# Decoder layer on one core: the down product of the seventh expert cut in two around the first gates of the eighth, and the last biases placed between the halves of the last down product

## The chip, the core and the metric

The kernel runs on one NeuronCore of a Trainium2 chip. The core has a matrix engine (TensorE, PE in the profile; its weight loads are listed as PEld), a vector engine (VectorE, DVE), a scalar engine (ScalarE, ACT), a general engine (GpSimd, POOL) and a queue that issues the DMAs (SyncE, SP). The metric is the time of one execution on the device in microseconds, as the median of repeated runs.

## What is computed

A decoder layer over 4 sequences of 256 tokens with 256 features: a state-space mixer, a small gate from a context, and then a feed-forward layer with experts. Only the last part matters here. For the layer-normed tokens `xt` (1024 of them) it is

```python
u = jnp.einsum('nh,ehi->eni', xt, Wup) + bup[:, None, :]
g = jax.nn.silu(jnp.einsum('eni,eij->enj', u, Wgate) + bgate[:, None, :]) * u
eo = jnp.einsum('enj,ejh->enh', g, Wdown) + bdown[:, None, :]
out = jnp.einsum('ne,enh->nh', probs, eo)
su = xt @ Wsu + bsu
sg = jax.nn.silu(su @ Wsg + bsg) * su
out = out + sg @ Wsd + bsd
```

There are 7 routed experts, of which each token weighs two with `probs`, and one shared expert that all tokens use. The kernel treats the shared one as an eighth (`NE` is 8, numbers 0 to 7), and runs every expert on every token.

## The kernel before

**Three products for an expert.** Up, gate and down are each a 256 by 256 product on 1024 tokens. Every 32-bit operand is split in a rounded high part and the rest of it (`uh` and `ul`, `eh` and `el`, `ewh` and `ewl` for weights), and a product is the sum of three passes: high by high, and the two mixed ones. Up and gate work on four blocks `v`, two halves of the tokens (512 each) by two halves of the features. A block is 6 matmuls of 512 columns into bank `v` (L1241 for the four with the high part of the moving side, L1244 for the two with the rest). Block 0 and block 1 belong to the first 512 tokens. Both need `uh` and `ul` of blocks 0 and 1 of the up product, because the gate sums over all features. Down works on eight tiles `t` of 128 tokens, 6 matmuls of 256 columns each (L1251), two tiles to a bank, banks 4 to 7.

**What the other engines do for one expert.** ACT adds the bias to the up result (`u32`, L909). DVE rounds it (`uh`, L1208), POOL subtracts (`ul`, L647). After the gate, ACT applies silu (`e32`, L930), DVE multiplies by `u32` (L1220), ACT rounds (`eh`, L925, in `round_e`), and POOL subtracts (`el`, L652). In the last expert DVE makes two of the four `el` blocks, 1 and 3 (L1225), to spare POOL, and POOL 0 and 2. DVE adds each down tile, weighed by `prob`, to the residual `xres` (`accumulate`, L1199), and the last expert's with L1191. In the profile `e32` and `u32` have the name `conv`, and `eh` the name `parts`, after the memory they lie in.

**The order of the work.** Each engine has its program in an order written out by hand, and waits on counting semaphores. The matrix engine's expert `e` is: up of `e`, down of `e - 1`, gate of `e`. Down of the last expert follows alone, and opens its banks with the weighed biases of all experts (8 matmuls, L1599), for which `acc_done` must show that the bank's tiles of the expert ahead have been added. `eh` has one buffer: `round_e` waits until the whole down product of the expert ahead has been read (`down_done` at `4 * e`). The down product of the last expert waits, at its tile 0 and its tile 4, for the two `el` blocks of that half (`el_done` from POOL, `el_last` from DVE). The output leaves in four DMAs, each after two tiles of L1191.

Of the kernel before, what the change touches and what calls it, by code (L numbers as in the profile page):

```python
# [56 lines left out]
def decoder_layer(nc, x, ctx_in, W_in, conv_w, conv_b, D, z_bias, W_out, xw, xb, Wr, br, gate_bias,  # L57
# [9 lines left out]
    with ExitStack() as stack:  # L67
# [597 lines left out]
        def _(act):  # L665
# [226 lines left out]
            def expert(e, k, q):  # L892
                first = isinstance(e, int) and e == 0
                if isinstance(e, int) and e == NE - 2:
                    for i in range(2):
                        act.wait_ge(prob_turned, i + 1)
                        act.copy(biasT[i], bank[4 + i][0:BIAS_ROWS, :]).then_inc(prob_read, 1)  # L897
                act.wait_ge(eb_done, e + 1)
                for v in range(4):
                    if first and v == 1:  # L900
                        root(slice(T + 4, 2 * T), 5)
                    if first and v == 2:
                        copy_logits(0)
                        split_turned(6, 6)
                        split_turned(7, 7)
                        act.preload_act_table(ACT.Silu)
                    act.wait_ge(up_done, 4 * e + v + 1)
                    at_least(act, e_done, 4 * (e - 1) + v + 1)
                    act.activation(u32[:, v, :], up_bank(e, v)[:], ACT.Identity,  # L909
                                   bias=eb[q][:, 0, v % 2:v % 2 + 1]).then_inc(up_read, 1)  # L910
                    if first:
                        act.wait_ge(up_read, v + 1)
                        act.copy(uh[:, v, :], u32[:, v, :]).then_inc(uh_done, 1)  # L913
                if first:
                    copy_logits(1)
                elif not (isinstance(e, int) and e == NE - 1):
                    at_least(act, down_done, 4 * e)
                    act.wait_ge(ew_in[1 - q], 48 * (k + q + 1))
                    for j in range(3):
                        split_weights(e + 1, 1 - q, j)  # L920

                def round_e(v):
                    act.wait_ge(e_done, 4 * e + v + 1)
                    at_least(act, down_done, 4 * e)
                    act.copy(eh[:, v, :], e32[:, v, :]).then_inc(eh_done, 1)  # L925

                for v in range(4):
                    act.wait_ge(gate2_done, 4 * e + v + 1)
                    at_least(act, el_done, 4 * (e - 1) + v + 1)
                    act.activation(e32[:, v, :], up_bank(e, v)[:], ACT.Silu,  # L930
                                   bias=eb[q][:, 1, v % 2:v % 2 + 1]).then_inc(silu2_done, 1)
                    if v:
                        round_e(v - 1)
                round_e(3)
                if first:

                    act.wait_ge(pexp_in, 1)
                    act.activation(lg[:], lg[:], ACT.Tanh).then_inc(pexp_done, 1)
# [5 lines left out]
        def _(dve):  # L944
# [247 lines left out]
                                             scalar=shift[:, t:t + 1], in1=xres[:, t, :],  # L1192
                                             op0=ALU.add, op1=ALU.add).then_inc(acc_done, 1)

            def accumulate(e):

                for t in range(T):
                    dve.wait_ge(down_done, 4 * e + t // 2 + 1)
                    dve.scalar_tensor_tensor(out=xres[:, t, :], in0=bank[4 + t // 2][:, DM * (t % 2):DM * (t % 2 + 1)],  # L1199
                                             scalar=prob[:, t, bass.ds(e, 1)], in1=xres[:, t, :],  # L1200
                                             op0=ALU.mult, op1=ALU.add).then_inc(acc_done, 1)

            def expert(e, k, q):
                first, second, final = (isinstance(e, int) and e == i for i in (0, 1, NE - 1))
                for v in range(4 * (not first)):
                    dve.wait_ge(up_read, 4 * e + v + 1)
                    at_least(dve, gate2_done, 4 * e)
                    dve.tensor_copy(uh[:, v, :], u32[:, v, :]).then_inc(uh_done, 1)  # L1208
                if not first:
                    accumulate(e - 1)  # L1210
                if not (first or final):
                    if second:
                        dve.wait_ge(ewl_done, 6)
                    for j in range(3):
                        rest_weights(e + 1, 1 - q, j)
                for v in range(4):
                    if first and v == 2:
                        compare()
                    dve.wait_ge(silu2_done, 4 * e + v + 1)
                    dve.tensor_tensor(e32[:, v, :], e32[:, v, :], u32[:, v, :], ALU.mult).then_inc(e_done, 1)  # L1220
                    if final and v >= 2:

                        w = 2 * v - 3
                        dve.wait_ge(eh_done, 4 * e + w + 1)
                        dve.tensor_tensor(el[:, w, :], e32[:, w, :], f32(eh[:, w, :]), ALU.subtract).then_inc(el_last, 1)  # L1225
                if first:
                    choose()
                    weigh_experts()
# [7 lines left out]
        def _(pe):  # L1236
# [353 lines left out]
                    high_first(up_bank(e, v)[:], [(w[q][:, 1, k, c], uh[:, 2 * n + k, :]) for k in range(KD) for w in (ewh, ewl)],  # L1590
                               [(ewh[q][:, 1, k, c], ul[:, 2 * n + k, :]) for k in range(KD)], before).then_inc(gate2_done, 1)

            def down(e, q):
                pe.wait_ge(ewl_done, 3 * e + 3)
                end = isinstance(e, int) and e == NE - 1
                for t in range(T * end):
                    if t % 2 == 0:
                        pe.wait_ge(acc_done, T * (e - 1) + t + 2)
                    pe.matmul(bank[4 + t // 2][:, DM * (t % 2):DM * (t % 2 + 1)], biasT[t // 4][:, t % 4 * P:(t % 4 + 1) * P], bd3[:],  # L1599
                              start=(t % 2 == 0), stop=False)  # L1600
                for t in range(T):
                    n = t // 4
                    if t % 4 == 0 and isinstance(e, int) and e == NE - 1:
                        pe.wait_ge(el_done, 4 * e + n + 1)
# [37 lines left out]
            def expert(e, k, q):  # L1642
                if isinstance(e, int) and e == 0:
                    up(0, 0, range(2))
                    logits(0)
                    turn_tokens(6, 6)
                    turn_tokens(7, 7)
                    gate(0, 0, range(2))
                    pe.wait_ge(lgT_read, 1)
                    up(0, 0, range(2, 4))  # L1650
                    logits(1)
                    turn_logits()
                    gate(0, 0, range(2, 4))
                else:
                    if isinstance(e, int) and e == NE - 2:
                        pe.wait_ge(acc_done, T * (NE - 3))
                        turn_prob()
                    up(e, q)
                    if isinstance(e, int) and e == NE - 2:
                        pe.wait_ge(prob_read, 2)  # L1660
                        pe.wait_ge(bd_done, 1)
                    down(e - 1, 1 - q)
                    gate(e, q)

            over_experts(pe, expert)
            down(NE - 1, 1)


# [27 lines left out]
```

## Time and profile before

| | us |
|---|---|
| median of 3 runs | 415.57 |
| lowest and highest | 415.22, 416.32 |
| profiled execution, its time | 417.49 |
| profiled execution, its span | 415.8 |

| engine | busy us | share of the span |
|---|---|---|
| PE | 392.3 | 94% |
| DVE | 333.7 | 80% |
| ACT | 227.4 | 55% |
| POOL | 176.8 | 43% |

The rows of the trace are times in us from the start of the span. The profiled execution took 1.69 us more than its span, for what lies around it, and was 1.92 us slower than the median of the unprofiled runs, so a change is reckoned as a difference in the span and laid on either time. The whole change lies in the last 22 us, from 393.7.

### The profile page before, as it was taken

The page shows a single profiled execution, that of the slowest core. Times are in us where ns is not written, and L with a number is a line of the kernel's source. Part 1 is how long each engine was busy: PE and PEld are TensorE (multiplying, and loading weights), DVE is VectorE, ACT ScalarE, POOL GpSimd, SP SyncE. Part 2 cuts the span into 40 slices and gives each one's busy share as a digit, 9 for nine tenths or more (in the row PEclk, how much of TensorE's full clock was granted, in tenths as well). Part 3 has the DMA queues.
Part 4 walks back from the last instruction along what each step waited for, and adds up shares of the span by engine and source line. Part 5 has one row for each costly group of instructions (what it writes and reads, how often), then busy time and mean ns, then how long its engine had stood idle before and what let it go on. Part 6 is the DMA issues. An engine that isn't in the chain of part 4 may idle for free.

```text
span 415.8 us, 8825 instructions
## 1 busy us (share of the span) xinstructions
PE 392.3 (94%) x2989; PEld 289.5 (70%) x2989; DVE 333.7 (80%) x565; ACT 227.4 (55%) x421; POOL 176.8 (43%) x208
## 2 busy tenths in 40 slices
PE   2899999999999999998999999599999999999996
PEld 1677666666667666664666667368897888978886
DVE  3687998999899998998988939819959678596685
ACT  5657455555555555558876631354555545555451
POOL 3699411011110111105546740226575865768561
PEclk9999999999999999999999999889999999999999
DMA  6402211322101221014231150000022020200002
GB/s 185 105 2 56 64 58 10 107 61 61 47 20 55 60 61 57 18 51 135 60 87 44 47 154 9 2 0 2 1 77 56 23 76 0 76 0 2 0 1 102
DMA packets 35932, 21.13 MB, mean 51 GB/s; under 512 B 17048, under 2 KB 33760, under 8 KB 35904
## 3 DMA queue, kind: packets, MB, share of 16 engines
q1 hardware_dynamic: 35904, 20.78, 17.7%
q8 instruction: 15, 0.25, 0.3%
q14 instruction: 13, 0.11, 0.1%
HBM read 18.13 MB, written 1.31 MB: 47 GB/s over the span
## 4 chain that ended last, share of the span: by engine, by line
PE 60%; DVE 18%; ACT 7%; issue 6%; POOL 5%; DMA 1%; DVEq 1%; ACTq 0%; SPq 0%; POOLq 0%
PE bank L1275 21%; PE bank L1468 7%; PE bank L1251 6%; POOL el L652 5%; PE bank L1388 4%; DVE conv L1012 4%; PE bank L1241 4%; DVE xres L1199 4%; PE bank L1456 3%; DVE conv L1220 2%; DVE ewl L1080 2%; PE bank L1261 2%; PE bank L1476 2%; PE bank L1415 2%; PE bank L1244 2%
## 5 line engine op out<-in xcount | busy, mean ns | idle before, releaser
L1012 DVE SCALAR_TENSOR_TENSOR conv<-bank,taps,conv 128x510 f32<-128x510 f32 (+2 forms) x204 | 150.8, 745 | 22.4 <-ACT conv L691 17.5
L1275 PE MATMUL bank<-uth,parts 128*128 128x512 f32 x272 | 96.7, 411 | 2.1 <-DVE utl L995 1.4
L691 ACT ACTIVATE conv<-bank,tap_b,taps 128x512 f32<-128x512 f32 x68 | 52.9, 778 | 57.3 <-PE bank L1275 57.2
L565 POOL TENSOR_TENSOR ce<-conv,ecx 128x512 f32<-128x512 f32 x15 | 19.4, 1295 | 123.1 <-DVE conv L1012 122.7
L1275 PEld LDWEIGHTS bank<-uth,parts 128*128 128x128 f32 x272 | 51.1, 188 | 16.3 <-DVE conv L1012 4.4
L647 POOL TENSOR_TENSOR ul<-conv,uh 128x512 fp32r<-128x512 f32 x32 | 42.9, 1358 | 42.3 <-ACT uh L913 29.3
L652 POOL TENSOR_TENSOR el<-conv,parts 128x512 fp32r<-128x512 f32 x30 | 44.3, 1504 | 30.3 <-ACT parts L925 30.3
L1275 PE MATMUL bank<-utl,parts 128*128 128x512 f32 x136 | 56.4, 415 | 0.0
L1208 DVE CAST uh<-conv 128x512 fp32r<-128x512 f32 x28 | 26.0, 967 | 22.5 <-ACT conv L909 22.3
L1095 DVE SCALAR_TENSOR_TENSOR g<-dec,bank 128x512 f32<-128x512 f32 x64 | 40.9, 679 | 1.7 <-PE bank L1388 1.7
L1220 DVE TENSOR_TENSOR conv<-conv 128x512 f32<-128x512 f32 x32 | 31.4, 1014 | 13.0 <-ACT conv L930 13.0
L1468 PEld LDWEIGHTS bank<-conv 64*128 64x128 f32 x512 | 31.1, 187 | 13.5 <-issue 11.1
L1468 PE MATMUL bank<-conv 64*128 64x128 f32 x512 | 37.2, 285 | 0.2
L1251 PE MATMUL bank<-ewh,parts 128*128 128x256 f32 x128 | 36.1, 282 | 0.7 <-ACT wzl L897 0.5
L1251 PE MATMUL bank<-ewl,parts 128*128 128x256 f32 x128 | 36.1, 282 | 0.0
L1251 PE MATMUL bank<-ewh,el 128*128 128x256 f32 x128 | 36.1, 282 | 0.0
L799 ACT ACTIVATE dec<-bank 128x512 f32<-128x512 f32 x64 | 34.5, 592 | 0.6 <-DVE g L1095 0.6
L925 ACT CAST parts<-conv 128x512 fp32r<-128x512 f32 x32 | 19.8, 618 | 27.6 <-DVE conv L1220 27.6
L1275 PEld LDWEIGHTS bank<-utl,parts 128*128 128x128 f32 x136 | 25.6, 189 | 8.6 <-issue 6.3
L909 ACT ACTIVATE conv<-bank,eb 128x512 f32<-128x512 f32 x32 | 19.7, 689 | 16.8 <-POOL eb L644 11.9
L930 ACT ACTIVATE conv<-bank,eb 128x512 f32<-128x512 f32 x32 | 21.9, 687 | 9.9 <-PE bank L1244 9.9
L1388 PE MATMUL bank<-g,xp 128*16 128x128 f32 x512 | 26.6, 278 | 0.0
(206 smaller groups left out, 732.1 us busy)
## 6 DMA issues: line engine op xcount, KB each, us to landing
w_raw<-in_L_attn_W_in_dram SPq DMA_DIRECT2D x17, 256.0 KB, 3.2
ecx<-ecum_dram SPq DMA_DIRECT2D x32, 128.0 KB, 2.9
ew_raw<-in_L_ffn_Wup_dram SPq DMA_DIRECT2D x7, 256.0 KB, 3.3
ew_raw<-in_L_ffn_Wgate_dram SPq DMA_DIRECT2D x7, 256.0 KB, 3.3
ew_raw<-in_L_ffn_Wdown_dram SPq DMA_DIRECT2D x7, 256.0 KB, 3.6
xres<-in_x_dram SPq DMA_DIRECT2D x2, 512.0 KB, 4.1
out_dram<-xres SPq DMA_DIRECT2D x4, 256.0 KB, 2.2
yi<-yev SPq DMA_DIRECT2D x56, 16.0 KB, 1.8
```

Source lines behind the costliest of these rows:

```text
L647: pool.tensor_tensor(ul[:, v, :], u32[:, v, :], f32(uh[:, v, :]), ALU.subtract).then_inc(ul_done, 1)
L652: pool.tensor_tensor(el[:, v, :], e32[:, v, :], f32(eh[:, v, :]), ALU.subtract).then_inc(el_done, 1)
L691: act.activation(conv[q][:, j, HALF * h:HALF * (h + 1)], bank[u % 2][:], ACT.Identity, bias=tap_b[q][:, j:j + 1], scale=taps[q][:, j, TAPS ...
L799: act.activation(dec[b][:], bank[4 + b][:], ACT.Exp).then_inc(exp_done, 1)
L1012: dve.scalar_tensor_tensor(out=dst[:, :, d:SEQ], in0=src[:, :, 0:SEQ - d], scalar=taps[q][:, j, TAPS - 1 - d:TAPS - d], in1=dst[:, :, d:SE ...
L1095: dve.scalar_tensor_tensor(out=g[b][:], in0=dec[b][:], scalar=1.0, in1=cb_bank(n, u // 2, b)[:], op0=ALU.min, op1=ALU.mult).then_inc(g_don ...
L1208: dve.tensor_copy(uh[:, v, :], u32[:, v, :]).then_inc(uh_done, 1)
L1220: dve.tensor_tensor(e32[:, v, :], e32[:, v, :], u32[:, v, :], ALU.mult).then_inc(e_done, 1)
L1251: ins = pe.matmul(dst, left, right, start=(k == 0 and i == 0 and not begun), stop=(ends and k == n - 1 and i == 2))
L1275: ins = pe.matmul(bank[u % 2][:], w, x_t, start=(i == 0), stop=(i == 3 * KD - 1))
L1388: ins = pe.matmul(y_bank(n, h)[32 * i:32 * i + 2 * HD, P * h:P * (h + 1)], xp[q][:, 4 * h + i, j, :], g[j][:, i * P:(i + 1) * P], start=fi ...
L1468: ins = pe.matmul(cb_bank(n, h, j)[:, i * P:(i + 1) * P], conv[q][r, 0, s], conv[q][r, 1, s], start=True, stop=True)
```

## The change

In the last expert (7), the down product of expert 6 is cut in two. The matrix engine now runs tiles 0 to 3 of it, the gate blocks 0 and 1 of expert 7, tiles 4 to 7, the biases of tiles 0 to 3, and then the gate blocks 2 and 3. The biases of tiles 4 to 7 move behind the first half of the last down product. The other engines follow. DVE adds the tiles 0 to 3 of expert 6 ahead of its products for the gate and the tiles 4 to 7 behind its first `el` block. It makes that block (1) ahead of the second half's products, where it stood behind the product of block 2. ACT rounds blocks 0 and 1 in a row and then 2 and 3 in a row, each pair behind the second silu of its half. No instruction is added or dropped.

```diff
@@ scalar engine, expert @@
+                    final = isinstance(e, int) and e == NE - 1
-                    if v:
+                    if v and not (final and v == 2):
                         round_e(v - 1)
+                    if final and v == 1:
+                        round_e(1)
                 round_e(3)
@@ vector engine @@
-            def accumulate(e):
-                for t in range(T):
+            def accumulate(e, tiles=range(T)):
+                for t in tiles:
                     dve.wait_ge(down_done, 4 * e + t // 2 + 1)
...
-                if not first:
+                if final:
+                    accumulate(e - 1, range(4))
+                elif not first:
                     accumulate(e - 1)
...
-                    if final and v >= 2:
-                        w = 2 * v - 3
+                    if final and v % 2:
+                        w = v
                         dve.wait_ge(eh_done, 4 * e + w + 1)
                         dve.tensor_tensor(el[:, w, :], e32[:, w, :], f32(eh[:, w, :]), ALU.subtract).then_inc(el_last, 1)
+                        if w == 1:
+                            accumulate(e - 1, range(4, T))
@@ matrix engine @@
+            def down_biases(tiles):
+                for t in tiles:
+                    if t % 2 == 0:
+                        pe.wait_ge(acc_done, T * (NE - 2) + t + 2)
+                    pe.matmul(bank[4 + t // 2][:, DM * (t % 2):DM * (t % 2 + 1)], biasT[t // 4][:, t % 4 * P:(t % 4 + 1) * P], bd3[:],
+                              start=(t % 2 == 0), stop=False)
...
-            def down(e, q):
+            def down(e, q, tiles=range(T)):
...
-                    down(e - 1, 1 - q)
-                    gate(e, q)
+                    if isinstance(e, int) and e == NE - 1:
+                        down(e - 1, 1 - q, range(4))
+                        gate(e, q, range(2))
+                        down(e - 1, 1 - q, range(4, T))
+                        down_biases(range(4))
+                        gate(e, q, range(2, 4))
+                    else:
+                        down(e - 1, 1 - q)
+                        gate(e, q)
...
-            down(NE - 1, 1)
+            down(NE - 1, 1, range(4))
+            down_biases(range(4, T))
+            down(NE - 1, 1, range(4, T))
```

The matrix engine in the last expert, before, from the last matmul of the seventh expert's down product. Bank 7 holds its tiles 6 and 7, banks 0 and 1 the gate blocks 0 and 1:

```order
L1251 MATMUL bank7<-ewh0,el 128x256
L1241 MATMUL bank0<-uh,ewh1 128x512 [waits uh_done,up_read,ewl_done]
L1241 MATMUL bank0<-uh,ewl1 128x512
L1241 MATMUL bank0<-uh,ewh1 128x512 [waits uh_done]
L1241 MATMUL bank0<-uh,ewl1 128x512
L1244 MATMUL bank0<-ul,ewh1 128x512 [waits ul_done] x2
L1241 MATMUL bank1<-uh,ewh1 128x512 [waits up_read]
```

The same gate in the changed kernel, with what stands ahead of it and behind it:

```order
L1258 MATMUL bank5<-ewh0,el 128x256
L1248 MATMUL bank0<-uh,ewh1 128x512 [waits uh_done,up_read,ewl_done]
L1248 MATMUL bank0<-uh,ewl1 128x512
L1248 MATMUL bank0<-uh,ewh1 128x512 [waits uh_done]
L1248 MATMUL bank0<-uh,ewl1 128x512
L1251 MATMUL bank0<-ul,ewh1 128x512 [waits ul_done] x2
L1248 MATMUL bank1<-uh,ewh1 128x512 [waits up_read]
L1248 MATMUL bank1<-uh,ewl1 128x512
L1248 MATMUL bank1<-uh,ewh1 128x512
L1248 MATMUL bank1<-uh,ewl1 128x512
L1251 MATMUL bank1<-ul,ewh1 128x512 x2
L1258 MATMUL bank6<-ewh0,parts 128x256 [waits acc_done,el_done,ewl_done]
```

The gate blocks 0 and 1 now stand behind bank 5, the first half of the down product, and banks 6 and 7 behind them.

The vector engine in the last expert, before. Banks 4 to 7 at L1199 are the tiles of expert 6, `conv1` is `e32`:

```order
L1199 SCALAR_TENSOR_TENSOR xres<-bank6,prob,xres 128x256 [waits down_done] x2
L1199 SCALAR_TENSOR_TENSOR xres<-bank7,prob,xres 128x256 [waits down_done] x2
L1220 TENSOR_TENSOR conv1<-conv1,conv0 128x512 [waits silu2_done] x3
L1225 TENSOR_TENSOR el<-conv1,parts 128x512 [waits eh_done]
L1220 TENSOR_TENSOR conv1<-conv1,conv0 128x512 [waits silu2_done]
L1225 TENSOR_TENSOR el<-conv1,parts 128x512 [waits eh_done]
```

And in the changed kernel (L1202 is the weighed addition, L1225 now the product, L1230 the subtraction for `el`):

```order
L1225 TENSOR_TENSOR conv1<-conv1,conv0 128x512 [waits silu2_done] x2
L1230 TENSOR_TENSOR el<-conv1,parts 128x512 [waits eh_done]
L1202 SCALAR_TENSOR_TENSOR xres<-bank6,prob,xres 128x256 [waits down_done] x2
L1202 SCALAR_TENSOR_TENSOR xres<-bank7,prob,xres 128x256 [waits down_done] x2
L1225 TENSOR_TENSOR conv1<-conv1,conv0 128x512 [waits silu2_done] x2
L1230 TENSOR_TENSOR el<-conv1,parts 128x512 [waits eh_done]
```

The last four weighed additions moved from ahead of all four products to between the second and the third, behind the first `el`.

## Rows read from the trace of the kernel before

**Rows 1.** The page: its span, and the engines on the chain that ended last.

```profile
span 415.8 us, 8825 instructions
...
PE 60%; DVE 18%; ACT 7%; issue 6%; POOL 5%; DMA 1%; DVEq 1%; ACTq 0%; SPq 0%; POOLq 0%
```

**Rows 2.** The chain that ended last, in order of time: start, us, what.

```profile
403.87 0.70 ACT conv L930
...
405.60 0.62 DVE el L1225
...
406.35 5.96 PE bank L1251 x48
...
412.33 0.48 DVE xres L1191
```

**Rows 3.** Timeline of PE, at 269 and from 393 on: start, us, operation, count, [idle].

```profile
269.55 1.97 PE L1291 MATMUL bank<-ident,xn 128*128 128x128 f32 x8 [4.67 <-DVE xn L988]
...
393.75 0.28 PE L1251 MATMUL bank<-ewh,parts 128*128 128x256 f32 x1
...
396.60 0.28 PE L1251 MATMUL bank<-ewh,parts 128*128 128x256 f32 x1
...
399.46 0.40 PE L1241 MATMUL bank<-uh,ewh 128*128 128x512 f32 x1
...
405.07 0.64 PE L1599 MATMUL bank<-bd,wzh 72*128 72x256 f32 x4
405.54 0.64 PE L1599 MATMUL bank<-bd,wzl 72*128 72x256 f32 x4
406.35 0.36 PE L1251 MATMUL bank<-ewh,parts 128*128 128x256 f32 x1 [0.16 <-DVE el L1225]
406.54 0.28 PE L1251 MATMUL bank<-ewl,parts 128*128 128x256 f32 x1
...
412.02 0.28 PE L1251 MATMUL bank<-ewh,el 128*128 128x256 f32 x1
```

**Rows 4.** Timeline of POOL and DVE from 395 to 402.3, the last expert.

```profile
397.47 1.40 POOL L647 TENSOR_TENSOR ul<-conv,uh 128x512 fp32r<-128x512 f32 x1 [0.36 <-DVE uh L1208]
...
399.08 3.21 DVE L1199 SCALAR_TENSOR_TENSOR xres<-bank,prob,xres 128x256 f32<-128x256 f32 x8
```

**Rows 5.** Timeline of POOL and PE in expert 2, gate blocks 0 and 1.

```profile
312.20 1.41 POOL L647 TENSOR_TENSOR ul<-conv,uh 128x512 fp32r<-128x512 f32 x1 [0.36 <-DVE uh L1208]
...
313.67 0.51 PE L1244 MATMUL bank<-ul,ewh 128*128 128x512 f32 x1 [0.33 <-POOL ul L647]
...
314.01 0.40 PE L1241 MATMUL bank<-uh,ewh 128*128 128x512 f32 x1
```

**Rows 6.** Timeline from 403 on: ACT, then DVE, then POOL.

```profile
403.06 0.61 ACT L925 CAST parts<-conv 128x512 fp32r<-128x512 f32 x1
...
406.83 0.63 ACT L925 CAST parts<-conv 128x512 fp32r<-128x512 f32 x1 [0.37 <-DVE conv L1220]
...
404.60 1.00 DVE L1220 TENSOR_TENSOR conv<-conv 128x512 f32<-128x512 f32 x1 [0.71 <-ACT conv L930]
405.52 0.68 DVE L1225 TENSOR_TENSOR el<-conv,parts 128x512 fp32r<-128x512 f32 x1
406.12 0.68 DVE L1220 TENSOR_TENSOR conv<-conv 128x512 f32<-128x512 f32 x1
407.49 1.01 DVE L1225 TENSOR_TENSOR el<-conv,parts 128x512 fp32r<-128x512 f32 x1 [0.69 <-ACT parts L925]
...
403.75 1.31 POOL L652 TENSOR_TENSOR el<-conv,parts 128x512 fp32r<-128x512 f32 x1 [2.18 <-ACT parts L925]
406.54 1.42 POOL L652 TENSOR_TENSOR el<-conv,parts 128x512 fp32r<-128x512 f32 x1 [1.49 <-ACT parts L925]
```

**Rows 7.** Stretches: busy us (count) by engine, granted TensorE clock, DMA share, GB/s.

```profile
270.00:272.00 2.00, 2.00 (x10) 1.90 (x9) 0.68 (x1) 1.03 (x2) 0.00 (x0) 0.50 0.00 0
```

**Rows 8.** The same view of the stretch of the last down product.

```profile
406.30:412.30 6.00, 5.95 (x48) 5.77 (x48) 4.05 (x8) 0.79 (x2) 1.42 (x1) 1.00 0.26 90
```

More of the change, by code:

```diff
@@ L1591, in gate @@
                                [(ewh[q][:, 1, k, c], ul[:, 2 * n + k, :]) for k in range(KD)], before).then_inc(gate2_done, 1)
-            def down(e, q):
+            def down_biases(tiles):
[5 more added lines that the diff above has]
+            def down(e, q, tiles=range(T)):
                 pe.wait_ge(ewl_done, 3 * e + 3)
                 end = isinstance(e, int) and e == NE - 1
[L1596 to L1601, printed above, removed]
+                for t in tiles:
                     n = t // 4
```

## The prediction

> **What bounds the kernel now.** I read the page first. The matrix engine holds 60% of the chain that ended last [rows 1]. The chain in order of time then says what ends the kernel: in the last 22 us it is matmuls, and it leaves them once, for silu, product and `el` block 1 on the vector engine, and comes back at 406.35 for the 48 matmuls of the last down product; from there a weighed addition and the output DMA follow [rows 2]. So the question is how well the matrix engine is filled from 393.75 to 412.02. Its timeline gives three paces. A down matmul takes a slot of 0.119 us: 24 of them lie between 393.75 and 396.60, which is 2.85. A gate matmul takes (405.07 - 399.46) / 24 = 0.234, so a block of 6 takes 1.40. Four biases take 0.47 (405.07 to 405.54). By these the engine is full except in one place. The biases are through at 405.54 + 0.47 = 406.01, and the last down product starts at 406.35 [rows 3]. That gap of **0.34 us** is all that a better order of the same matmuls can win here.
>
> **What the change is after.** It puts 24 matmuls of the seventh expert's down product between the first and the second pair of gates, so that silu, product, `eh` and `el` of the first half get more time before the last down product. Nothing is added to any engine, so each engine's busy time stays. Three things move, and each must be set against the moment at which its input is there.
>
> **Part 1, the first gates come 2.85 us earlier.** The first half of the down product starts at 393.75 as before and ends at 396.60 [rows 3]. Gate block 0 then starts instead of at 399.46. Its last matmul needs `ul` block 1, which POOL makes from 397.47 to 398.87 [rows 4]. Nothing ahead of it is moved by the change, so it stays there. Before, that matmul was due at 399.46 + 5 x 0.234 = 400.63 and found it ready 1.8 us long. Now it is due at 397.77. The trace has the same meeting in expert 2: `ul` block 1 from 312.20 to 313.61, the matmul that waits for it at 313.67, the next one at 314.01 [rows 5]. With these steps, 0.06 and 0.34, the waiting matmul starts at 398.93 and block 1 at 399.27. It was due at 396.60 + 1.40 = 398.00. The **first stall is 1.27 us**. Behind it are queued, on the same engine, block 1 and the second half of the down product. Block 0 may also wait for `uh` block 1, but that was there when POOL began at 397.47, so this wait lies within the other.
>
> **Part 2, the second half of the down product comes later.** It runs from 399.27 + 1.40 = 400.67 to 403.52, where before it was over at 399.46. The four biases that follow need tiles 0 to 3 of expert 6 added. The vector engine adds 8 tiles in 3.21 from 399.08 [rows 4], 0.39 each behind the first, so four are done by 400.8, and that costs nothing. But ACT rounds no `eh` block before the whole down product has been read, and that is now so only after 403.40, the start of its last matmul. From a down matmul to an engine that waits for it I take 412.33 - 412.02 = 0.31 [rows 2, 3]. So the rounding of block 0 starts at 403.71, though its silu is over by about 400.1 (0.4 behind the matmul of 398.93, and 0.70 long) and its product by 402.8, even if it starts behind the additions and takes twice the 1.00 us of [rows 6]. It started at 403.06 before.
>
> **Part 3, the vector engine's new order.** From 403.71 I follow one chain with the durations of [rows 6]:
> - two roundings by ACT, 0.61 each. The first ends at 404.32, and POOL starts `el` block 0 0.08 later (403.06 + 0.61 to 403.75), at 404.40, for 1.31, to 405.71.
> - `el` block 1 on the vector engine is asked for at 404.96, while POOL runs. What happens then stands in the rows: the product at 404.60 lasted 1.00 instead of 0.68, and the next instruction came at 405.52, 0.46 after POOL ended (405.06). So the next instruction starts at 405.71 + 0.46 = 406.17. Block 1 itself is through by 406.25. The matrix engine wants it only after the gates, at 403.52 + 0.47 + 12 x 0.234 = 406.80. No stall there: the aim of the change is met, with 0.4 us to spare.
> - the four weighed additions of tiles 4 to 7 stand now in front of the second half's products: 4 x 0.39 = 1.57, to 407.74. Before they were done before 402.3, beside gates, and cost nothing. That cover is gone.
> - product of block 2: 0.68, to 408.42. Its silu is no limit, since gate block 2 ends near 405.4 and silu takes 0.70 [rows 2]. Rounding of block 2: 0.03 later (406.80 to 406.83), 0.61, to 409.06. `el` block 2 on POOL: 409.14, 1.31, to 410.45.
> - the product of block 3 and its rounding end at about 409.7, so `el` block 3 on the vector engine meets POOL once more. Such an `el` ended 0.54 after POOL (407.49 + 1.01 against 406.54 + 1.42). It ends at 410.99.
> - the matrix engine started 0.15 after such an end (405.52 + 0.68 to 406.35). The second half of the last down product starts at 411.14.
>
> The matrix engine would be ready at 406.80 + 2.85 + 0.47 = 410.12. So the **second stall is 1.02 us**.
>
> **The sum.** The last matmul starts 0.19 + 22 x 0.119 = 2.81 after 411.14 [rows 3], at 413.95, against 412.02: **+1.93 us**. The stalls alone say nearly the same: 1.27 + 1.02 - 0.34 = 1.95. The tail behind the last matmul is not changed: two additions and one DMA of two tiles, since the tiles still come two by two at the same pace. On the profiled execution that makes 415.8 + 1.9 = 417.7 of span and 417.49 + 1.93 = 419.4 of time. On the median of the runs it makes 415.57 + 1.93 = **417.5 us**. A measurement of this kernel can tell about 0.3%, 1.25 us, from no change, and 1.93 is above that.
>
> **Bounds.** The first stall rests on a row of the very same meeting, 0.1 either way. The second is a sum of ten steps behind the first one. Its lower bound is zero, if a step or two of the chain are shorter by 1.02 in all. Its upper bound is from rows where POOL's subtraction is held up: it took 1.42 beside the vector engine's product instead of 1.31 [rows 6]. If that happened at both of POOL's `el` blocks and the products met POOL as at 404.60 (+0.32 each), it would be 0.22 + 0.64 = 0.9 more. I take the middle, since in my chain both of POOL's blocks start while the vector engine waits.
>
> The rows show that the vector engine's two-input operations end half a microsecond after POOL's, not at their own pace. The Trainium skill, page "SBUF — State Buffer", section "SBUF: two separate sides", has a rule for it: VectorE and GpSimd share a port pair, "the shared pair is an exclusive lock", and who starts first holds it for its whole instruction. It speaks against this change, which hands the last `el` of each half to the vector engine right behind POOL's. Without such a lock the chain would be 0.6 shorter at block 1 (0.68 from 404.96 on) and would end with POOL's block 2 near 409.9, and the second stall would be gone. That is the first rival.
>
> **Rivals.**
> - **Only the first stall is paid.** The vector engine and POOL do not hold each other up, or the additions slip in earlier, and the last half is ready by 410.12. Then the time is 415.57 + 1.27 - 0.34 = 416.5, not slower by what can be measured. For it: the chain decides only by 1.02 us, and ten steps are in it. Against it: both meetings have their rows [rows 6].
> - **The change does what it is after.** If `ul` block 1 were there by 397.77, there would be no first stall, and everything behind it would come 1.27 earlier as well, except what counts from the gates. Then at most the gap of 0.34 is won: 415.2. It decides at 1.1 us of earlier `ul`. Against it: the two times stand in the trace, and nothing ahead of them moves.
> - **The clock falls.** Two stalls of over 1 us could cost the matrix engine its clock. Where it was granted 0.50, at 1.2 GHz, it made 10 matmuls in 2 us [rows 7]; that was after idling for 4.67 us [rows 3]. At the end it is granted 1.00 [rows 8]. At half the pace the last 24 matmuls take 2.85 more: 420.4. Against it: each stall is about a quarter of that idling, and the gap of today left the clock at 1.00.
> - **POOL is held up too**: the upper bound, 417.5 + 0.9 = 418.4.
>
> **How the numbers follow.** Forecast 0.70; only the first stall 0.15; does what it is after 0.04; POOL held up 0.08; the clock 0.03. Faster by over 0.3% can't come from the order at all (at most 0.34 us), so it gets 0.01 for the spread of the runs. Slower by over 0.3% gets the forecast, less a little where measured spread eats the 0.7 between 1.93 and 1.25, and the two worse cases: 0.77. Within it: 0.22. The range goes from 416.3, which takes in the first rival, to 418.8, which takes in the last one with some spread. What it leaves out holds less than 0.2.
>
> **What would show it.** In the changed kernel's timeline the matmul for `ul` block 1 stands near 398.9 after 1.2 us of idling; ACT's two roundings start near 403.7, close behind one another; `el` block 1 on the vector engine lasts about 1.3; the biases of tiles 4 to 7 start near 409.65; and the matrix engine idles for about 1 us before 411.1, released by `el` block 3. The idle time before 406.35 is gone. I am wrong if the first stall is under 1 us, or if the second half of the last down product starts right behind its biases.

## The result, and the profile after

| | median us | lowest to highest | runs |
|---|---|---|---|
| kernel before | 415.49 | 414.87 to 416.32 | 5 |
| changed kernel | 417.58 | 416.90 to 417.94 | 5 |

The changed kernel takes 1.0042 of the time before, with a 95% interval of 1.0025 to 1.0060. That ratio is 1.7 us, and its interval 1.0 to 2.5; the two medians lie 2.1 us apart. The forecast was +1.93, to 417.5.

The span alone would mislead. The page of the changed kernel says 415.9 against 415.8 in [rows 1], because this execution had an earlier start. The first weights came from memory 1.16 us sooner, as the first matmul of each timeline shows (before, then after):

```profile
8.03 1.08 PE L1261 MATMUL bank<-ident,w_raw 128*128 128x128 f32 x4 [8.03 <-DMA w_raw<-in_L_attn_W_in_dram]
```

```profile
span 415.9 us, 8824 instructions
...
6.87 1.09 PE L1268 MATMUL bank<-ident,w_raw 128*128 128x128 f32 x4 [6.87 <-DMA w_raw<-in_L_attn_W_in_dram]
```

By the last expert the whole trace is 1.87 us earlier. So I compare the stretch that the change touches, from the first matmul of the seventh expert's down product to the last matmul of all. Before it is 393.75 to 412.02, **18.27 us** [rows 3]. In the changed kernel the timeline of PE shows (start, us, operation, count, [idle before and who ended it]):

```profile
391.88 0.28 PE L1258 MATMUL bank<-ewh,parts 128*128 128x256 f32 x1
...
394.74 0.40 PE L1248 MATMUL bank<-uh,ewh 128*128 128x512 f32 x1
...
395.58 0.51 PE L1248 MATMUL bank<-uh,ewh 128*128 128x512 f32 x1 [0.21 <-DVE uh L1211]
...
397.06 0.51 PE L1251 MATMUL bank<-ul,ewh 128*128 128x512 f32 x1 [0.50 <-POOL ul L647]
397.40 0.39 PE L1248 MATMUL bank<-uh,ewh 128*128 128x512 f32 x1
...
404.94 0.28 PE L1258 MATMUL bank<-ewh,parts 128*128 128x256 f32 x1
...
407.79 0.65 PE L1605 MATMUL bank<-bd,wzl 72*128 72x256 f32 x4
409.31 0.36 PE L1258 MATMUL bank<-ewh,parts 128*128 128x256 f32 x1 [0.88 <-DVE el L1230]
...
412.11 0.28 PE L1258 MATMUL bank<-ewh,el 128*128 128x256 f32 x1
```

That is 412.11 - 391.88 = **20.23 us**, 1.96 more. There are two stalls. Gate block 1 was due at 394.74 + 1.40 = 396.14 and starts at 397.40: 1.26 us, begun by the wait for `uh` block 1 and ended by `ul` block 1. The second half of the last down product was due at 407.79 + 0.47 = 408.26 and starts at 409.31, 1.05 us late, released by the vector engine's `el`. The gap of 0.34 before the last down product is gone: its first half starts at 404.94, right behind the gates, and no idle time is noted there.

The other engines in the same stretch (timelines of DVE, ACT and POOL):

```profile
403.07 1.37 DVE L1230 TENSOR_TENSOR el<-conv,parts 128x512 fp32r<-128x512 f32 x1 [2.22 <-ACT parts L925]
404.36 1.65 DVE L1202 SCALAR_TENSOR_TENSOR xres<-bank,prob,xres 128x256 f32<-128x256 f32 x4
405.93 1.28 DVE L1225 TENSOR_TENSOR conv<-conv 128x512 f32<-128x512 f32 x2
407.89 1.27 DVE L1230 TENSOR_TENSOR el<-conv,parts 128x512 fp32r<-128x512 f32 x1 [0.69 <-ACT parts L925]
...
401.90 1.14 ACT L925 CAST parts<-conv 128x512 fp32r<-128x512 f32 x2 [2.21 <-PE bank L1258]
...
402.59 1.29 POOL L652 TENSOR_TENSOR el<-conv,parts 128x512 fp32r<-128x512 f32 x1 [2.90 <-ACT parts L925]
407.34 1.28 POOL L652 TENSOR_TENSOR el<-conv,parts 128x512 fp32r<-128x512 f32 x1 [3.45 <-ACT parts L925]
```

ACT's roundings start at 401.90 and were released by the matmuls of the down product, after 2.21 us of idling. Each `el` of the vector engine (403.07 for 1.37, 407.89 for 1.27) begins while one of POOL's is under way. The four additions stand between.

### The profile page after: what moved, and what is told of

It is laid out like the page before. It is cut to its first block, busy times and chain, and to the rows that moved or that the text cites. A ratio compares the mean times of both kernels' runs of the same rounds, so it can differ in the third digit from the quotient of the medians.

```text
span 415.9 us, 8824 instructions
## 1 busy us (share of the span) xinstructions
PE 392.7 (94%) x2989; PEld 289.6 (70%) x2989; DVE 334.8 (81%) x565; ACT 227.4 (55%) x421; POOL 176.5 (42%) x208
## 4 chain that ended last, share of the span: by engine, by line
PE 67%; DVE 15%; ACT 6%; POOL 5%; issue 4%; DMA 1%; SPq 0%; DVEq 0%; ACTq 0%; POOLq 0%
PE bank L1282 22%; PE bank L1475 7%; PE bank L1258 7%; PE bank L1248 7%; PE bank L1395 4%; POOL el L652 4%; PE bank L1251 4%; PE bank L1463 3%; DVE conv L1015 3%; DVE xres L1202 3%; PE bank L1268 2%; PE bank L1483 2%; PE bank L1422 2%; PE bank L1443 2%; DVE conv L1225 1%
## 5 line engine op out<-in xcount | busy, mean ns | idle before, releaser
L1225 DVE TENSOR_TENSOR conv<-conv 128x512 f32<-128x512 f32 x32 | 31.6, 1027 | 12.4 <-ACT conv L930 12.3
```

## The experiments

The theory: two stalls in a row, each with its own cause. The first is the first gates being put ahead of `ul` block 1. The second is the chain from the end of the split down product through rounding, POOL, the vector engine's `el`, four additions and the second half's products. The rivals: one chain only, in which what one stall gives up the other takes; POOL and the vector engine not in each other's way; a loss from the followers' new order and not from the cut. In every table of runs the last column but one is the stretch defined above, in one profiled execution, and the last one its difference to 18.27.

**1. Cut at tile 6.** This takes away the first cause alone.

```diff
-                        down(e - 1, 1 - q, range(4))
+                        down(e - 1, 1 - q, range(6))
                         gate(e, q, range(2))
-                        down(e - 1, 1 - q, range(4, T))
+                        down(e - 1, 1 - q, range(6, T))
```

> The changed kernel with the cut of the seventh expert's down product at tile 6 in place of tile 4, nothing else. Theory (two stalls in a row, each from its own cause): the first gates come 1.42 us later, so the matmul that needs ul block 1 is due 1.42 later, after ul is there, and the first stall of 1.27 us goes. The second stall stays at about 1.0, since the chain behind the down product starts earlier by as much as the matrix engine is ready earlier. Sum against the kernel before: 1.02 - 0.34 = +0.7 us (measured for the changed kernel: +1.97 in the last expert). Rival A (one chain only: what the first stall costs, the second would cost without it): about +2 again, with a second stall of 2.3. Rival B (the loss has nothing to do with this order): +2 and the same stalls.

Timeline of PE of this kernel:

```profile
391.61 0.28 PE L1258 MATMUL bank<-ewh,parts 128*128 128x256 f32 x1
...
396.83 0.64 PE L1251 MATMUL bank<-ul,ewh 128*128 128x512 f32 x2
398.24 0.62 PE L1251 MATMUL bank<-ul,ewh 128*128 128x512 f32 x2
...
406.26 0.65 PE L1605 MATMUL bank<-bd,wzl 72*128 72x256 f32 x4
407.79 0.36 PE L1258 MATMUL bank<-ewh,parts 128*128 128x256 f32 x1 [0.88 <-DVE el L1230]
410.59 0.28 PE L1258 MATMUL bank<-ewh,el 128*128 128x256 f32 x1
```

The two matmuls for `ul` are one pair now and nobody waits for POOL; the next pair follows 1.41 later. The second stall is what it was: due at 406.26 + 0.47 = 406.73, started at 407.79, 1.06 late. So the stalls are independent, and the first is worth 1.25 us. Rival A, that the second would take what the first gives, falls, and so does rival B, by which both stalls would have stayed.

**2. The additions ahead of the first `el`.** The vector engine idles 2.22 us there in the changed kernel.

```diff
                     if final and v % 2:
                         w = v
+                        if w == 1:
+                            accumulate(e - 1, range(4, T))
                         dve.wait_ge(eh_done, 4 * e + w + 1)
                         dve.tensor_tensor(el[:, w, :], e32[:, w, :], f32(eh[:, w, :]), ALU.subtract).then_inc(el_last, 1)
-                        if w == 1:
-                            accumulate(e - 1, range(4, T))
```

> The changed kernel with the vector engine's four weighed additions of tiles 4 to 7 ahead of its first el block instead of behind it, where the vector engine idles for 2.2 us. Theory: they leave the chain between the first el and the second half's products. Silu of block 3 then sets the pace, and the second stall falls from 1.05 to about 0.3; the first stays at 1.26. Sum against before: 1.27 + 0.27 - 0.34 = +1.2 us. Rival A (the second stall comes from POOL and the vector engine holding each other up, the additions are hidden by it): +1.95, second stall still 1.0.

**3. Rounding not held back by the whole down product.** Tiles 0 to 3 are the only readers of `eh` blocks 0 and 1, so it is enough for these two to wait for `down_done` at `4 * e - 2`.

```diff
-                    at_least(act, down_done, 4 * e)
+                    at_least(act, down_done, 4 * e - 2 * (isinstance(e, int) and e == NE - 1 and v < 2))
                     act.copy(eh[:, v, :], e32[:, v, :]).then_inc(eh_done, 1)
```

> The changed kernel, but ACT's rounding of blocks 0 and 1 in the last expert waits only for the first half of the seventh expert's down product (tiles 0 to 3 are the only ones that read these two blocks), not for the whole. Theory: rounding starts about 1.6 us earlier, at 402.1 on the clock of the kernel before; el block 1 and the additions end 1.6 earlier, silu of block 3 sets the pace, the second stall falls from 1.05 to about 0.3, the first stays. Sum against before: +1.2 us. Rival A (the additions wait for the second half of the down product anyway, and keep the chain where it is): +1.95.

The timelines of PE of the second kernel and of the third, each from the start of the stretch:

```profile
392.18 0.28 PE L1258 MATMUL bank<-ewh,parts 128*128 128x256 f32 x1
...
397.32 0.49 PE L1251 MATMUL bank<-ul,ewh 128*128 128x512 f32 x1 [0.51 <-POOL ul L647]
...
408.05 0.65 PE L1605 MATMUL bank<-bd,wzl 72*128 72x256 f32 x4
408.67 0.35 PE L1258 MATMUL bank<-ewh,parts 128*128 128x256 f32 x1
...
411.47 0.28 PE L1258 MATMUL bank<-ewh,el 128*128 128x256 f32 x1
```

```profile
392.40 0.28 PE L1258 MATMUL bank<-ewh,parts 128*128 128x256 f32 x1
...
397.58 0.50 PE L1251 MATMUL bank<-ul,ewh 128*128 128x512 f32 x1 [0.51 <-POOL ul L647]
...
408.30 0.65 PE L1605 MATMUL bank<-bd,wzl 72*128 72x256 f32 x4
...
411.72 0.28 PE L1258 MATMUL bank<-ewh,el 128*128 128x256 f32 x1
```

Both keep the first stall as it was and lose most of the second. In the second kernel the last half starts at 408.67, 0.15 after the biases were through (408.05 + 0.47 = 408.52), where the stall was 1.05. The two edits give the same, 19.29 and 19.32, though one shortens the chain at its middle and the other at its head. That fits one chain which in both is overtaken by silu of block 3, and ACT and the vector engine show it in the second kernel: the product of block 3 waits for that silu, and the rounding of block 2 stands right behind it.

```profile
405.41 0.69 ACT L930 ACTIVATE conv<-bank,eb 128x512 f32<-128x512 f32 x1 [0.71 <-PE bank L1251]
405.99 0.61 ACT L925 CAST parts<-conv 128x512 fp32r<-128x512 f32 x1
...
406.13 0.69 DVE L1225 TENSOR_TENSOR conv<-conv 128x512 f32<-128x512 f32 x1 [0.71 <-ACT conv L930]
```

Rival A of either expectation wanted +1.95 and falls. The additions cost 0.94 us where the change put them, and nothing 2 us earlier.

**4. `el` block 2 on the vector engine.** POOL makes one block less, the vector engine one more.

```diff
-                for v in ((0, 2) if isinstance(e, int) and e == NE - 1 else range(4)):
+                for v in ((0,) if isinstance(e, int) and e == NE - 1 else range(4)):
@@ vector engine @@
                         w = v
+                        if w == 3:
+                            dve.wait_ge(eh_done, 4 * e + 3)
+                            dve.tensor_tensor(el[:, 2, :], e32[:, 2, :], f32(eh[:, 2, :]), ALU.subtract)
@@ matrix engine @@
-                        pe.wait_ge(el_done, 4 * e + n + 1)
+                        pe.wait_ge(el_done, 4 * e + 1)
```

> The changed kernel with el block 2 made by the vector engine instead of POOL: one 128x512 subtraction more for the vector engine, one less for POOL, so the vector engine makes blocks 2 and 3 one behind the other and meets POOL in neither. Theory (the vector engine's subtraction can't run while POOL's does, and ends 0.5 us after it): el block 3 is ready 0.65 us earlier, second stall about 0.4, first stall unchanged. Sum against before: +1.3 us. Rival (the two engines don't hold each other up, 1.27 us is the length of the work): the vector engine has two of them in a row and block 3 comes no earlier, +1.95 to +2.5.

Timelines of DVE and PE of this kernel. L1231 and L1233 are the two subtractions:

```profile
404.35 1.37 DVE L1233 TENSOR_TENSOR el<-conv,parts 128x512 fp32r<-128x512 f32 x1 [2.24 <-ACT parts L925]
...
408.58 0.69 DVE L1231 TENSOR_TENSOR el<-conv,parts 128x512 fp32r<-128x512 f32 x1
409.19 0.68 DVE L1233 TENSOR_TENSOR el<-conv,parts 128x512 fp32r<-128x512 f32 x1
...
393.17 0.28 PE L1261 MATMUL bank<-ewh,parts 128*128 128x256 f32 x1
...
410.02 0.36 PE L1261 MATMUL bank<-ewh,parts 128*128 128x256 f32 x1 [0.30 <-DVE el L1233]
412.82 0.28 PE L1261 MATMUL bank<-ewh,el 128*128 128x256 f32 x1
```

The same subtraction takes 1.37 us while POOL runs its own, and 0.68 and 0.69 while POOL is idle. More work on the vector engine made the stretch shorter by 20.23 - 19.65 = 0.58 us. In direction this agrees with the rule cited in the prediction from the Trainium skill, page "SBUF — State Buffer", section "SBUF: two separate sides". In size it does not quite: an engine blocked until the other's whole instruction is over would end 0.68 after POOL, and in the changed kernel the second `el` ended 409.16 - 408.62 = 0.54 after it. The ends given for POOL are rough, so what makes up the 0.14 stays open.

| run | median us | before, same runs | ratio, 95% interval | stretch us | to before |
|---|---|---|---|---|---|
| 1 cut at tile 6 | 416.60 | 415.64 | 1.0023 (1.0008 to 1.0037) | 18.98 | +0.71 |
| 2 additions first | 416.94 | 415.64 | 1.0026 (1.0011 to 1.0041) | 19.29 | +1.02 |
| 3 rounding early | 416.90 | 415.64 | 1.0023 (1.0011 to 1.0035) | 19.32 | +1.05 |
| 4 `el` 2 on DVE | 417.34 | 415.64 | 1.0036 (1.0022 to 1.0050) | 19.65 | +1.38 |

Each kernel has 12 runs, against 35 of the kernel before. By the times alone the four can't be told from one another: their intervals overlap, and all four overlap that of the changed kernel (1.0025 to 1.0060). The order among them, and what each edit wins, rests on the stretches, one profiled execution each.

**5. The followers' order without the cut.** The matrix engine's part and the additions go back to the order before. Rounding of blocks 0 and 1 in a row, and `el` block 1 ahead of the second half's products, stay.

```diff
-                if final:
-                    accumulate(e - 1, range(4))
-                elif not first:
+                if not first:
                     accumulate(e - 1)
...
-                        if w == 1:
-                            accumulate(e - 1, range(4, T))
@@ matrix engine @@
-                        down(e - 1, 1 - q, range(4))
-                        gate(e, q, range(2))
-                        down(e - 1, 1 - q, range(4, T))
-                        down_biases(range(4))
-                        gate(e, q, range(2, 4))
+                        down(e - 1, 1 - q)
+                        gate(e, q)
+                        down_biases(range(T))
...
-            down(NE - 1, 1, range(4))
-            down_biases(range(4, T))
-            down(NE - 1, 1, range(4, T))
+            down(NE - 1, 1)
```

> The matrix engine's order and the weighed additions as in the kernel before, and only ACT's and the vector engine's new order for the blocks of the last expert: eh 0 and 1 rounded in a row behind the second silu, el block 1 made ahead of the products of blocks 2 and 3. Theory (the seventh expert's down product should not have been cut; the gap of 0.34 us was the late el block 1): el block 1 is ready 0.6 us earlier, before the biases are through, the gap before the last down product goes, and el block 3 is just in time for its second half. -0.3 to -0.4 us against before, first and second stall both absent. Rival A (the followers' order does the damage, not the cut): +1 us or more. Rival B (the early rounding holds up silu of block 2 and with it the second half): 0, with a new stall of up to 0.4 inside the last down product.

Timelines of DVE and PE of this kernel:

```profile
404.21 1.02 DVE L1228 TENSOR_TENSOR el<-conv,parts 128x512 fp32r<-128x512 f32 x1 [0.69 <-ACT parts L925]
405.16 1.28 DVE L1223 TENSOR_TENSOR conv<-conv 128x512 f32<-128x512 f32 x2
407.13 1.29 DVE L1228 TENSOR_TENSOR el<-conv,parts 128x512 fp32r<-128x512 f32 x1 [0.69 <-ACT parts L925]
...
393.39 0.28 PE L1254 MATMUL bank<-ewh,parts 128*128 128x256 f32 x1
...
405.19 0.64 PE L1601 MATMUL bank<-bd,wzl 72*128 72x256 f32 x4
...
408.56 0.36 PE L1254 MATMUL bank<-ewh,parts 128*128 128x256 f32 x1
...
411.37 0.28 PE L1254 MATMUL bank<-ewh,el 128*128 128x256 f32 x1
```

The stretch is 17.98, 0.29 shorter than before. The gap went, since `el` block 1 ended at 405.23, ahead of the last bias (405.19 + 0.47 = 405.66). `el` block 3 met POOL and was just late: the last down product's second half was due at 405.66 + 2.85 = 408.51 and began at 408.56. It also lost 0.07 in its first slot, which is longer behind a wait (0.19 in [rows 3], 406.35 to 406.54, against 0.119). So the followers' order does no damage (rival A), and wins most of what the cut was meant to win. Rival B is half right: ACT starts silu of block 2 only at 404.09, 10.70 into the stretch where it was 10.12 before (403.87 - 393.75). But the product of block 2 stands behind `el` block 1 in any case, until 405.16, and the stretch is shorter all the same.

ACT's new order and the vector engine's were not taken apart. By [rows 6] the vector engine's alone might do: rounding of block 1 ended at 404.46 + 0.61 = 405.07 and POOL's block 0 at 405.06, so an `el` block 1 right behind them would let the matrix engine go at about 405.07 + 0.03 + 0.68 + 0.15 = 405.93, ahead of 406.01. That is an estimate, and no run shows it.

**6. The biases alone.** The kernel before, with the biases of tiles 4 to 7 between the halves of the last down product.

```diff
-            down(NE - 1, 1)
+            down_biases(range(4))
+            down(NE - 1, 1, range(4))
+            down_biases(range(4, T))
+            down(NE - 1, 1, range(4, T))
```

> The kernel before with one part of the change alone: the biases of tiles 4 to 7 between the halves of the last down product. Theory: the matrix engine reaches the last down product 0.47 us earlier, waits for the same el block 1 until 406.35 as before, with a gap of 0.81 in place of 0.34, and then pays the 0.47 of biases between the halves, since el block 3 is there by then: +0.47 us, in the last expert's length. Rival (a bias moved into a gap is won): 0 or -0.3.

Timeline of PE of this kernel:

```profile
392.87 0.28 PE L1251 MATMUL bank<-ewh,parts 128*128 128x256 f32 x1
...
404.19 0.64 PE L1597 MATMUL bank<-bd,wzh 72*128 72x256 f32 x4
405.46 0.36 PE L1251 MATMUL bank<-ewh,parts 128*128 128x256 f32 x1 [0.64 <-DVE el L1225]
...
411.59 0.28 PE L1251 MATMUL bank<-ewh,el 128*128 128x256 f32 x1
```

The wait for `el` block 1 is 405.46 - (404.19 + 0.47) = 0.80 instead of 0.34, and the four biases are paid between the halves, at 408.39. In the kernel before they had filled a wait. In the changed kernel no run tests their new place by itself. There they stand ahead of the second stall, in which the matrix engine waits until 409.31 for `el` block 3 and not for them.

**7. All four mends together**, on the changed kernel.

```diff
-                        down(e - 1, 1 - q, range(4))
+                        down(e - 1, 1 - q, range(6))
...
+                        if w == 1:
+                            accumulate(e - 1, range(4, T))
+                        if w == 3:
+                            dve.wait_ge(eh_done, 4 * e + 3)
+                            dve.tensor_tensor(el[:, 2, :], e32[:, 2, :], f32(eh[:, 2, :]), ALU.subtract)
...
+                    at_least(act, down_done, 4 * e - 2 * (isinstance(e, int) and e == NE - 1 and v < 2))
```

The lines of edit 4 for POOL and for the matrix engine's wait are in it too.

> The changed kernel with all four mends of the first batch: cut at tile 6, additions ahead of the first el block, rounding of blocks 0 and 1 behind the first half of the down product only, el block 2 on the vector engine. Theory: both stalls go, and the gap of before as well: -0.34 us in the last expert against before, which is all that this kind of order can win, too little to be told from no change in the time. Rival (the split costs something of its own on the matrix engine, a switch between down and gate each time): +0.3 or more without any stall that a row names.

```profile
390.89 0.28 PE L1261 MATMUL bank<-ewh,parts 128*128 128x256 f32 x1
...
406.01 0.28 PE L1261 MATMUL bank<-ewh,parts 128*128 128x256 f32 x1
...
408.73 0.28 PE L1261 MATMUL bank<-ewh,el 128*128 128x256 f32 x1
```

The stretch is 17.84, 0.43 shorter than before. That is what the slots alone add up to, 95 x 0.119 + 24 x 0.234 + 0.94 for the eight biases = 17.86, so the matrix engine idles nowhere in it. A switch between down and gate costs nothing of its own, and the rival falls. It also shows that a cut of the down product need not cost anything: the losses were those of its place and of what stood around it. And the gap of before was worth more than its 0.34 us: 18.27 - 17.86 = 0.41, because the first matmul behind a wait takes 0.07 longer.

**8. The followers' order and `el` block 2 on the vector engine**, which is edit 5 with edit 4.

```diff
+                        if w == 3:
+                            dve.wait_ge(eh_done, 4 * e + 3)
+                            dve.tensor_tensor(el[:, 2, :], e32[:, 2, :], f32(eh[:, 2, :]), ALU.subtract)
...
+                        down(e - 1, 1 - q)
+                        gate(e, q)
+                        down_biases(range(T))
```

> As the kernel with the followers' order alone, and el block 2 made by the vector engine too. Theory: as that kernel, -0.34 us in the last expert, with more room before the second half of the last down product (block 3 ready about 0.6 us earlier). If el block 3 was late in the other kernel by up to 0.1, that goes. Rival: the vector engine is the bound in the second half, and the last down product stalls in the middle by 0.2 or more.

The stretch is 17.86, so the 0.12 that was left in 5 went as well.

**9 and 10. The changed kernel and kernel 8 once more**, with no edit of their own.

> The changed kernel once more, on one chip with the two best variants. Theory: +1.96 us in the last expert's length, and a median 1.5 to 2.4 us above the kernel before. If the first measurement (+2.1) owed part to the spread of the runs, this one comes out nearer to +1.96 or below; under +1.25 would mean that the time does not follow the last expert's length.

> The kernel with the followers' order and el block 2 on the vector engine once more. Theory: the same -0.41 us in the last expert's length, and a median 0.1 to 0.8 us under the kernel before; with the first set of runs together this may or may not be told from zero.

| run | median us | before, same runs | ratio, 95% interval | stretch us | to before |
|---|---|---|---|---|---|
| 5 followers only | 415.50 | 415.86 | 0.9988 (0.9972 to 1.0003) | 17.98 | -0.29 |
| 6 biases only | 416.57 | 415.86 | 1.0021 (1.0007 to 1.0036) | 18.72 | +0.45 |
| 7 all mended | 415.47 | 415.86 | 0.9988 (0.9975 to 1.0002) | 17.84 | -0.43 |
| 8 followers, `el` 2 on DVE | 415.28 | 415.86 | 0.9988 (0.9973 to 1.0002) | 17.86 | -0.41 |
| 9 changed, again | 418.02 | 416.05 | 1.0046 (1.0031 to 1.0060) | 20.19 | +1.92 |
| 10 kernel 8, again | 416.14 | 416.05 | 0.9995 (0.9980 to 1.0010) | 17.86 | -0.41 |

The intervals of 5, 7, 8 and 10 all lie below both of the changed kernel's (from 1.0025 and from 1.0031), so these are faster than it. Against the kernel before they are not: all intervals hold 1. The 0.4 us shows in the stretch, which repeats well (17.86 in both 8 and 10, 20.23 and 20.19 for the changed kernel), but a median of 12 runs does not resolve it: the second set for kernel 8 came out at +0.09 us, where -0.1 to -0.8 was expected.

## Why the prediction was right

Its own steps, laid beside the changed kernel. The times of after are moved by 1.87, the lead that this execution had at the start of the stretch.

| step | predicted | measured | after, moved |
|---|---|---|---|
| first stall | 1.27 | 1.26 | |
| matmul for `ul` block 1 | 398.93 | 397.06 | 398.93 |
| rounding of block 0 | 403.71 | 401.90 | 403.77 |
| `el` block 0 on POOL | 404.40 | 402.59 | 404.46 |
| additions start | 406.17 | 404.36 | 406.23 |
| products start | 407.74 | 405.93 | 407.80 |
| `el` block 2 on POOL | 409.14 | 407.34 | 409.21 |
| second half of the last down | 411.14 | 409.31 | 411.18 |
| second stall | 1.02 | 1.05 | |
| last matmul | 413.95 | 412.11 | 413.98 |
| difference of the stretch | +1.93 | +1.96 | |

- **The matmul that is held up was found in another expert.** [rows 5] had the meeting of POOL and the matrix engine with its two small steps, and the stall came out to 0.01. Experiment 1 took this cause away and 1.25 us went.
- **The chain behind the split down product** was right in each of its links. Experiments 2, 3 and 4 each took away one (0.94, 0.91 and 0.58 us). For 2 and 3, I had forecast +1.2 and got +1.02 and +1.05. What was mis-sized there is ACT's pace: a rounding right behind a silu starts 0.1 before the silu's end (in experiment 2 the silu runs from 405.41 for 0.69 and the rounding starts at 405.99), where I had set one behind the other. That is 0.1 of the 0.15 to 0.18 that I missed; the rest was not traced. In the changed kernel two roundings took 1.14 and not 1.22, but that lay beside POOL's `el` block 0 and cost nothing.
- **The first rival**, that the second stall is hidden, falls with experiment 4: the two engines do hold each other up, and by the amount in [rows 6] (the vector engine's `el` ends 0.54 after POOL's there, and 0.56 and 0.54 after it in the changed kernel). The last rival did not come either: POOL's two `el` blocks took 1.29 and 1.28, so POOL was not held up.
- **The clock** stayed. The stretches of the changed kernel with the stalls have a granted clock of 1.00 (the column after POOL's busy time):

```profile
394.70:398.80 4.10, 3.39 (x15) 2.14 (x13) 4.10 (x8) 1.14 (x2) 3.73 (x4) 1.00 0.00 0
...
407.80:409.30 1.50, 0.63 (x6) 0.44 (x5) 1.41 (x2) 0.06 (x1) 0.82 (x1) 1.00 0.00 0
409.30:412.40 3.10, 3.08 (x24) 2.88 (x24) 2.31 (x6) 0.00 (x0) 0.00 (x0) 1.00 0.48 163
```

- **What was wrong** is the number for the profiled execution. I laid +1.93 on the span of one execution and forecast 417.7, and it was 415.9. That execution's head was 1.87 us shorter, of which 1.16 is the first load from memory. By the waits that both timelines of PE show, the lead is 1.15 at 17.82 us (16.67 in the changed kernel), 2.13 at 193.16 (191.03) and 1.78 at 280.30 (278.52), all of it in work that the change does not touch; why it grows and shrinks there stays open. A difference that is reckoned in one stretch can be checked only in that stretch.
- **Too small** was the 0.34 us as "all that a better order of the same matmuls can win". Kernels 7, 8 and 10 won 0.43 and 0.41. The price of the gap is the idle time and the longer first slot behind it, 0.34 + 0.07. The forecast did not suffer, since the changed kernel has such a slot too, behind its second stall.
- That the median came within 0.1 us of the forecast is partly luck: single runs of either kernel spread over 1 us and more, and the second set of runs gave +1.97 where the first gave +2.09.

The aim of the change itself was met. The first half of the last down product no longer waits for its `el`. But that wait was worth 0.41 us, and to fill it with the seventh expert's matmuls in this way meant that something else came too early (the gates, for `ul`) or too late (the down product's end, for rounding).

## What to carry to other kernels

Before a block of work is moved into a gap, note when the inputs of everything that it pulls forward are ready, and who waits for the end of what it pushes back: here 0.41 us could be won and each side lost more than 1. Try first to bring the late operand forward on the engine that makes it. A new order of ACT and the vector engine closed the gap, with the matrix engine's left as it was. A wait that guards a whole buffer where only half of it is reused is free as long as the buffer's reader ends early, and becomes part of the chain once that reader is split and ends late: here the rounding of `eh` waited for the end of the whole down product, and freeing it won 0.91 us.

## What the runs showed that I had not expected

Back to back on ACT, a 128x512 operation starts about 0.1 us before the end that the profile gives for the one ahead. This is a third of the gap that the change was after. Two executions with the same program up to there had their first matmul at 6.87 and at 8.03 us, by the first load from memory alone. That is more than half of what the change costs, and nearly three times what the best order wins. So a change of this size is read from the stretch, not from the span.
